# Unit rows by VectorE and their upper parts by ScalarE; a PSUM bank for each task and the last norm's transposes behind down products, in a fused attention and feed-forward kernel

## The chip, the cores and the metric

The kernel runs on one core of one Trainium2 chip. The time is the device time of one execution in microseconds; a verdict compares the kernel before and the changed kernel by such times. TensorE (PE in the profile) multiplies matrices, VectorE (DVE) and ScalarE (ACT) do element-wise work and can read PSUM, the banks that TensorE writes; GpSimd (POOL) does element-wise work on SBUF only; SyncE (SP) issues the DMAs.

## The reference

For each of 16 sequences of 128 tokens with 256 features, cross attention with 32 heads of 8 and then a gated feed-forward layer of 704 hidden units with integer weights, both added to x through a tanh gate:

```python
def _rmsnorm(t):
    return t * jax.lax.rsqrt(jnp.mean(t * t, axis=-1, keepdims=True) + EPS)
q = _rmsnorm(heads(layernorm(x) @ Wq.T)); k = _rmsnorm(heads(context @ Wk.T)); v = heads(context @ Wv.T)
attn = jax.nn.softmax(jnp.einsum('bhnd,bhmd->bhnm', q, k) * scale, axis=-1)
x = x + jnp.tanh(g_xattn[0]) * einsum(attn, v)
gate = silu(_qlinear(layernorm(x), wq_gate, s_gate)); up = _qlinear(layernorm(x), wq_up, s_up)
x = x + jnp.tanh(g_ffn[0]) * _qlinear(gate * up, wq_down, s_down)
```

(`heads` stands here for the reshape into 32 heads.)

## The kernel before

A tile is one sequence (128 tokens by 256 features); the 16 tiles make 8 pairs (`PAIRS`), since the feed-forward layer works on 256 tokens at once. Each engine runs its own list of instructions, written out by hand as an `iteration(p)` for p = -1 to 9 (p = 3 to 5 are a loop, the others are unrolled); semaphores join the lists. An iteration has two halves, e = 0 and e = 1, one for each tile of the pair. It is software pipelined: iteration p projects queries and keys of tiles 2p+2 and 2p+3, does the attention of tiles 2p and 2p+1 in four octets of heads each, normalises tiles 2p-1 and 2p for the feed-forward layer, does chunks 0 and 1 of the feed-forward layer (`ffn0`, `ffn1`) of pair p-1, and chunks 2 to 5 and the down products (`y0`, `y1`) of pair p-2. So iteration 8 has no projections and scores left, and iteration 9 only the last pair's chunks 2 to 5 and its down products. In those two the kernel drains.

Operands of the large products are split into an upper part of reduced precision and a lower part (the rest), and each product is made of both. For queries and keys the chain is: TensorE projects (line 1326); ScalarE squares (`square`) and copies (`copy_qk`, L658, to `qk_raw`); VectorE sums the squares (L942), adds epsilon and takes the inverse root in an 8-step chain `root_y` (L903, L809 to L815) that also holds the layer norm's variance; `normalize2` (L915) writes `x1n`, the normalised tile for the feed-forward layer; `normalize` (L858) writes `xn` for a later tile's queries. Then the unit rows are made twice from `qk_raw` and `root_y`: by VectorE as f16 into `qk_parts` (`qk_upper`, L955), and by GpSimd in full precision into `qk_unit` (`qk_norm`, L530). GpSimd subtracts the two (`split_qk`, L476), VectorE doubles the parts (`qk_double`, L967 and L969), and two transposing DMAs of SyncE bring them to `q_stack` and `k_stack`, from which TensorE takes the scores most of an iteration later.

For each chunk of the feed-forward layer TensorE fills a bank (L1392), ScalarE takes the tanh (L686), VectorE makes `silu2` (`gate`, L1018) and `hidden` (`up`, L1034, which frees the bank), ScalarE rounds it (`upper`, L697) and GpSimd makes the lower part (`split_hidden`, L488). The down products (L1421, L1439) need both parts.

GpSimd's list in the second half of an iteration is, in order: `qk_norm`, `split_qk`, then for two finished tiles a scaling and an addition (`add_y`, L516 and L518), then `add_attention` (L507) for the next iteration's first tile, for whose statistics VectorE waits (L1005).

PSUM has eight banks: four for scores (`score_ps`), one for the weighted values (`pv_ps`), and three that go round among 17 tasks by the table `BANK_OF`. `claim` makes TensorE wait until the task before in the same bank has been drained. In iterations 8 and 9 that table is the same, though nobody needs the four score banks any more. `keep_warm(n)` issues n products of an identity matrix that nobody reads.

## Time and profile before

| what | value |
|---|---|
| median of 3 runs | 254.87 us (253.89 to 255.37) |
| the profiled execution's own time | 252.63 us |
| its span, first to last instruction | 250.4 us |
| mean granted TensorE clock | 0.923 of full |
| busy: PE, DVE, ACT, POOL | 209.6, 193.1, 165.0, 121.9 us |

The profiled execution lies 0.5% below the fastest of the three runs; 2.2 us of its time lie outside the span. PEclk is the clock that TensorE was granted, 1.00 being 2.4 GHz and 0.50 being 1.2 GHz. Matmuls overlap, so PE's busy time says when it worked, not how hard.

### The profile page before, as it was taken

What the parts mean: (1) busy time and instruction counts of PE and PEld (TensorE: products, weight loads), DVE (VectorE), ACT (ScalarE), POOL (GpSimd) and SP (SyncE); (2) the same over time, 40 slices, a digit from 0 to 9 for tenths busy, and PEclk for the clock granted to TensorE, in tenths of its full rate; (3) what the DMA queues carried; (4) which work ended last, traced back from release to release, by engine and by line L of the source; (5) the groups of instructions that cost most, each with busy time, mean ns of one, the idle gap of its engine ahead of it and who ended that gap; (6) DMA issues with size and microseconds to landing.
All of it is one profiled execution on the core that took longest, in us unless ns stands there. A gap on an engine that the chain in (4) does not pass through costs nothing.

```text
span 250.4 us, 7077 instructions
## 1 busy us (share of the span) xinstructions
PE 209.6 (84%) x2536; PEld 171.3 (68%) x2536; DVE 193.1 (77%) x574; ACT 165.0 (66%) x311; POOL 121.9 (49%) x160
## 2 busy tenths in 40 slices
PE   7694875688399899979997999799998998982973
PEld 7592753466178687849885888588777876862963
DVE  4799499798976989696959795969698977686163
ACT  4458599466258886785588768755987588553260
POOL 6211343423424645755484649462946473644442
PEclk9996599589779999997999999979999999997699
DMA  5999405040807040604050405040623150000001
GB/s 168 286 395 339 94 3 85 5 82 7 86 3 86 1 86 1 130 3 84 3 127 0 83 0 126 0 83 1 63 65 67 19 116 16 23 23 0 21 22 45
DMA packets 39692, 17.82 MB, mean 71 GB/s; under 512 B 32752, under 2 KB 39024, under 8 KB 39536
## 3 DMA queue, kind: packets, MB, share of 16 engines
q1 hardware_dynamic: 39664, 17.45, 31.3%
q8 instruction: 18, 0.29, 0.5%
q14 instruction: 10, 0.08, 0.1%
HBM read 7.48 MB, written 2.10 MB: 38 GB/s over the span
## 4 chain that ended last, share of the span: by engine, by line
DVE 36%; PE 27%; issue 17%; POOL 8%; ACT 6%; DMA 2%; SPq 2%; DVEq 1%; POOLq 0%; ACTq 0%
PE bank L1326 8%; PE pv_ps L1294 5%; PE bank L1421 4%; PE bank L1392 4%; DVE sums L942 4%; DVE hidden L1034 3%; DVE qk_parts L955 3%; DVE silu L1018 3%; POOL y_sb L516 2%; DMA w_raw<-w_qkv_dram 2%; POOL x_all L507 2%; PE bank L1362 2%; PE score_ps L1275 2%; DVE root_y L811 2%; DVE root_y L903 2%
## 5 line engine op out<-in xcount | busy, mean ns | idle before, releaser
L594 ACT ACTIVATE probs<-score_ps 128x1024 f32<-128x1024 f32 x64 | 66.1, 1035 | 5.8 <-PE score_ps L1275 5.8
L1294 PE MATMUL pv_ps<-probs,v_blocks 128*32 128x128 f32 x1024 | 43.3, 287 | 8.8 <-ACT probs L594 5.9
L1392 PE MATMUL bank<-x_hi,gu_hi 128*128 128x256 f32 x176 | 46.8, 301 | 2.0 <-DVE hidden L1034 2.0
L530 POOL TENSOR_TENSOR qk_unit<-qk_raw,root_y 128x512 f32<-128x512 f32 x15 | 17.4, 1158 | 57.7 <-DVE root_y L815 57.7
L1392 PE MATMUL bank<-x_lo,gu_hi 128*128 128x256 f32 x176 | 44.0, 285 | 0.0
L488 POOL TENSOR_TENSOR h_lo<-hidden,h_hi 128x256 fp32r<-128x256 f32 x40 | 31.3, 794 | 15.9 <-ACT h_hi L697 15.9
L1392 PEld LDWEIGHTS bank<-x_hi,gu_hi 128*128 128x128 f32 x176 | 34.3, 195 | 6.1 <-issue 2.6
L1294 PEld LDWEIGHTS pv_ps<-probs,v_blocks 128*32 128x32 f32 x1024 | 25.0, 112 | 16.3 <-ACT probs L594 9.1
L1326 PE MATMUL bank<-w_hi,xc_hi 128*128 128x256 f32 x96 | 31.7, 330 | 3.5 <-POOL w_lo L559 1.8
L1392 PEld LDWEIGHTS bank<-x_lo,gu_hi 128*128 128x128 f32 x176 | 34.3, 195 | 0.0
L686 ACT ACTIVATE tanh_g<-bank,half_gate 128x256 f32<-128x256 f32 (+1 forms) x48 | 22.7, 472 | 17.3 <-PE bank L1392 15.5
L1275 PE MATMUL score_ps<-q_stack,k_stack 32*128 32x128 f16 x512 | 26.0, 223 | 5.4 <-ACT k_stack L777 3.2
L1326 PE MATMUL bank<-w_lo,xc_hi 128*128 128x256 f32 x96 | 29.6, 309 | 0.0
L1326 PE MATMUL bank<-w_hi,xc_lo 128*128 128x256 f32 x96 | 29.5, 308 | 0.0
L1018 DVE SCALAR_TENSOR_TENSOR silu<-tanh_g,bank 128x256 f32<-128x256 f32 (+1 forms) x48 | 19.9, 416 | 11.3 <-ACT tanh_g L686 10.7
L1275 PEld LDWEIGHTS score_ps<-q_stack,k_stack 32*128 32x128 f16 x512 | 14.8, 95 | 19.2 <-issue 12.9
L1326 PEld LDWEIGHTS bank<-w_hi,xc_hi 128*128 128x128 f32 x96 | 20.7, 215 | 7.8 <-DVE xc_lo L932 2.5
L1034 DVE SCALAR_TENSOR_TENSOR hidden<-silu,scales,bank 128x256 f32<-128x256 f32 (+1 forms) x48 | 23.0, 480 | 2.0
L476 POOL TENSOR_TENSOR qk_parts<-qk_unit,qk_parts 128x512 f16<-128x512 f32 x15 | 17.6, 1172 | 13.7 <-DVE qk_parts L955 13.6
L1421 PE MATMUL bank<-dn_hi,h_hi 128*128 128x256 f32 x84 | 23.8, 317 | 0.0
L697 ACT CAST h_hi<-hidden 128x256 fp32r<-128x256 f32 (+1 forms) x48 | 18.4, 407 | 8.2 <-DVE hidden L1034 7.8
L1326 PEld LDWEIGHTS bank<-w_hi,xc_lo 128*128 128x128 f32 x96 | 20.9, 218 | 0.0
(105 smaller groups left out, 440.6 us busy)
## 6 DMA issues: line engine op xcount, KB each, us to landing
out_dram<-x_all SPq DMA_DIRECT2D x16, 128.0 KB, 2.0
gu_int<-w_gu_dram SPq DMA_DIRECT2D x1, 1536.0 KB, 8.8
x_all<-x_dram SPq DMA_DIRECT2D x1, 1280.0 KB, 14.4
ctx_sb<-ctx_dram SPq DMA_DIRECT2D x1, 1280.0 KB, 17.5
w_raw<-w_qkv_dram SPq DMA_DIRECT2D x3, 256.0 KB, 3.3
dn_int<-w_dn_dram SPq DMA_DIRECT2D x1, 768.0 KB, 10.1
x_all<-x_dram SPq DMA_DIRECT2D x2, 256.0 KB, 5.3
ctx_sb<-ctx_dram SPq DMA_DIRECT2D x1, 512.0 KB, 6.5
```

The lines of the kernel that those rows point to most:

```text
L476: nc.gpsimd.tensor_tensor(lower_parts(), qk_unit[:].rearrange("p (s h) d -> p s h d", s=2), qk_parts[:, :, 0, :].rearrange("p (s h) d -> p ...
L488: nc.gpsimd.tensor_tensor(lower, hidden[of, j % 3, :], h_hi[of, j, :].bitcast(F32), ALU.subtract).then_inc(h_lo_ready, 1)
L594: nc.scalar.activation(probs[:, t % 2, :], score_ps[t % 2][:].rearrange("p h n -> p (h n)"), ACT.Exp, scale=float(HD) ** 0.5 / UNIT ** 2). ...
L686: nc.scalar.activation(tanh_g[0:r, j % 2, :], bank[k][0:r, 0:TOK], ACT.Tanh, scale=half_gate[0:r, j:j + 1]).then_inc(tanh_g_ready, 1)
L697: nc.scalar.copy(h_hi[of, j, :], hidden[of, j % 3, :]).then_inc(h_hi_ready, 1)
L1018: nc.vector.scalar_tensor_tensor(out=silu2[hidden_rows(j), j % 2, :], in0=tanh_g[0:r, j % 2, :], scalar=1.0, in1=bank[k][0:r, 0:TOK], op0= ...
L1034: nc.vector.scalar_tensor_tensor(out=hidden[of, j % 3, :], in0=silu2[of, j % 2, :], scalar=scales[of, 2, j:j + 1], in1=bank[k][of, half], ...
L1275: last = nc.tensor.matmul(score_ps[t % 2][:, s, :], k_stack[of, e, g, :], q_stack[of, e, g, :], start=True, stop=True, tile_position=(BLOC ...
L1294: last = nc.tensor.matmul(pv_ps[BLOCK * quadrant:BLOCK * (quadrant + 1), region * P:(region + 1) * P], v_blocks[:, e, h * BLOCK:(h + 1) * ...
L1326: last = nc.tensor.matmul(dst, a[:, tile, KC * source + c, :], w[:, column, c, :], start=(n == 1), stop=(n == 3 * KC))
L1392: last = nc.tensor.matmul(bank[k][:, a * TOK:(a + 1) * TOK], w[:, j, a, c, :], xx[:, c, :], start=(n == 1), stop=(n == (4 if wide_weights ...
L1421: last = nc.tensor.matmul(bank[k][:, 0:D], hh[:, j, e * P:(e + 1) * P], w[:, j, :], start=(j == 0 and n == 0), stop=(j == NJ - 1 and n == ...
```

## The change

It has two parts.

1. **Unit rows.** `qk_norm` moves from GpSimd to VectorE, where it takes the place of `qk_upper`: VectorE writes `qk_unit` (f32) once, and ScalarE rounds it to f16 into `qk_parts` with a new `qk_hi`. On ScalarE that copy stands, for e = 0, behind the first exponential of the second half and ahead of chunk 5's tanh; for e = 1, between the tanh of chunk 0 and that of chunk 1. In the second half VectorE's `qk_norm` now stands ahead of `normalize` instead of behind it.
2. **The last two iterations.** TensorE's lists for p = 8 and 9 are replaced by one, `last_pairs`. The four score banks join the ring of three (`NBANK` = 7, `LAST_BANK_OF`). Pair 6's down products now stand partly ahead of `turn2(8)` (the transposes of the last pair's `x1n`) and partly around chunks 0 and 1 of the last pair; 6 warm-up products stand ahead of `turn2(8)` and 5 behind it. VectorE takes all seven root steps of tile 15 in one piece and writes `x1n` ahead of chunks 3 and 4; `turn2_lo` comes ahead of chunk 5. Pair 6's outputs are scaled and added by VectorE at the very end (`add_last_pairs`) instead of by ScalarE and GpSimd.

```diff
-WARM = (14, 14)
+WARM = (14, 14, 6, 5)
...
+    RING, NBANK = 3, 7
+    LAST_BANK_OF = ({"out0": 2, "ffn2": 1, "ffn3": 3, "ffn4": 0, "ffn5": 4, "turn2": 2, "y0": 5, "y1": 6, "ffn0": 1, "ffn1": 3},
+                    {"ffn2": 0, "ffn3": 4, "ffn4": 2, "ffn5": 1, "y0": 3, "y1": 0})
...
+            def qk_hi(p, e):
+                b = 2 * p + e
+                if not has_tile(p, b + 2) or isinstance(b, int) and b == -2:
+                    return
+                act.wait_ge(unit_ready, b + 3)
+                if since(b, -1):
+                    act.wait_ge(stacked, 32 * (b + 2))
+                nc.scalar.copy(qk_parts[:, :, 0, :], qk_unit[:]).then_inc(qk_hi_ready, 1)
...
                 exp_octet(p, 1, 0)
+                if not (isinstance(p, int) and p == FIRST):
+                    qk_hi(p, 0)
                 tanh_chunk(p, 2, 5)
...
                 tanh_chunk(p, 1, 0)
+                qk_hi(p, 1)
                 tanh_chunk(p, 1, 1)
...
-            def qk_upper(p, e):
+            def qk_norm(p, e):
...
                 if since(b, -1):
-                    dve.wait_ge(stacked, 32 * (b + 2))
-                nc.vector.tensor_tensor(qk_parts[:, :, 0, :], qk_raw[:], root_y[:, 0:2 * H].unsqueeze(2).to_broadcast([P, 2 * H, HD]),
-                                        ALU.mult).then_inc(qk_hi_ready, 1)
+                    dve.wait_ge(qk_lo_ready, b + 2)
+                nc.vector.tensor_tensor(qk_unit[:], qk_raw[:], root_y[:, 0:2 * H].unsqueeze(2).to_broadcast([P, 2 * H, HD]),
+                                        ALU.mult).then_inc(unit_ready, 1)
...
+            def last_pairs(wide_weights):
+
+                p = PAIRS
+                weigh(p, 0, 0)
+                out_rows(p, 0)
+                for j in (2, 3, 4, 5):
+                    chunk(p, j, wide_weights)
+                down_part(p, (0, 1, 2), wide_weights)
+                keep_warm(WARM[2])
+                turn2(p)
+                keep_warm(WARM[3])
+                chunk(p, 0, wide_weights)
+                down_part(p, (3, 4), wide_weights)
+                chunk(p, 1, wide_weights)
+                down_part(p, (5,), wide_weights)
+                for j in (2, 3, 4, 5):
+                    chunk(p + 1, j, wide_weights)
+                down_part(p + 1, (0, 1, 2, 3), wide_weights)
+                down_part(p + 1, (4,), wide_weights)
+                down_part(p + 1, (5,), wide_weights)
```

`down_part(p, chunks, ...)` makes the products of these chunks for both tiles of the pair, and waits for each chunk's lower part.

How the rows stand on the engines now. ScalarE, iteration 6, around the first exponential of the second half; before:

```order
L594 ACTIVATE probs<-score_ps1 128x1024
L697 CAST h_hi<-hidden 128x256
L686 ACTIVATE tanh_g<-bank0,half_gate 128x256
L602 COPY o_turned<-pv_ps 128x384
L594 ACTIVATE probs<-score_ps0 128x1024
L686 ACTIVATE tanh_g<-bank1,half_gate 64x256
```

and of the change, the same place:

```order
L590 ACTIVATE probs<-score_ps1 128x1024
L702 CAST h_hi<-hidden 128x256
L691 ACTIVATE tanh_g<-bank0,half_gate 128x256
L598 COPY o_turned<-pv_ps 128x384
L590 ACTIVATE probs<-score_ps0 128x1024
L663 CAST qk_parts<-qk_unit 128x64x8
L691 ACTIVATE tanh_g<-bank1,half_gate 64x256
```

The rounding copy of the unit rows stands between the exponential and chunk 5's tanh, and so ahead of the turned tile (`xc_hi`) and of the next exponential too.

VectorE, iteration 8, from the roots of tile 15 on (L1018 and L1034 are `gate` and `up` of chunks 3, 4 and 5; L1051 is `turn2_lo`); before:

```order
L811 SCALAR_TENSOR_TENSOR root_y<-root_v,root_y 128x65
L1034 SCALAR_TENSOR_TENSOR hidden<-silu2,scales,bank2 128x256
L812 SCALAR_TENSOR_TENSOR root_xy<-root_in,root_y 128x65
L813 SCALAR_TENSOR_TENSOR root_v<-root_xy,root_y 128x65
L814 SCALAR_TENSOR_TENSOR root_p<-root_v 128x65
L815 SCALAR_TENSOR_TENSOR root_y<-root_p,root_y 128x65
L915 SCALAR_TENSOR_TENSOR x1n<-x_all,x1_mean_var,root_y 128x256
L1018 SCALAR_TENSOR_TENSOR silu2<-tanh_g,bank0 128x256
L1034 SCALAR_TENSOR_TENSOR hidden<-silu2,scales,bank0 128x256
L1018 SCALAR_TENSOR_TENSOR silu2<-tanh_g,bank1 64x256
L1034 SCALAR_TENSOR_TENSOR hidden<-silu2,scales,bank1 64x256
L1051 TENSOR_TENSOR x2_lo<-bank1,x2_hi 128x512
```

and of the change (L926 writes `x1n`, L1029 and L1045 are `gate` and `up`, L1062 is `turn2_lo`):

```order
L824 SCALAR_TENSOR_TENSOR root_v<-root_xy,root_y 128x65
L825 SCALAR_TENSOR_TENSOR root_p<-root_v 128x65
L826 SCALAR_TENSOR_TENSOR root_y<-root_p,root_y 128x65
L926 SCALAR_TENSOR_TENSOR x1n<-x_all,x1_mean_var,root_y 128x256
L1029 SCALAR_TENSOR_TENSOR silu2<-tanh_g,score_ps0 128x256
L1045 SCALAR_TENSOR_TENSOR hidden<-silu2,scales,score_ps0 128x256
L1029 SCALAR_TENSOR_TENSOR silu2<-tanh_g,bank0 128x256
L1045 SCALAR_TENSOR_TENSOR hidden<-silu2,scales,bank0 128x256
L1062 TENSOR_TENSOR x2_lo<-bank2,x2_hi 128x512
L1029 SCALAR_TENSOR_TENSOR silu2<-tanh_g,score_ps0 64x256
L1045 SCALAR_TENSOR_TENSOR hidden<-silu2,scales,score_ps0 64x256
```

`gate` and `up` of chunk 3 went from between the root steps to behind `x1n`, and `turn2_lo` went from behind chunk 5 to ahead of it.

TensorE, iteration 8, around the transposes of the last pair's `x1n`, which write bank 1 right behind chunk 5 in the same bank; before:

```order
L1392 MATMUL bank1<-x2_hi,gu_hi 128x256
L1392 MATMUL bank1<-x2_lo,gu_hi 128x256
L1373 MATMUL bank1<-ident,x1n 128x128 x4
L1421 MATMUL bank2<-dn_hi,h_hi 128x256
L1421 MATMUL bank2<-dn_hi,h_lo 128x256
L1421 MATMUL bank2<-dn_hi,h_hi 128x256
```

and of the change, where `score_ps1` holds pair 6's outputs and bank 2 the transposes:

```order
L1449 MATMUL score_ps1<-dn_hi,h_hi 128x256
L1449 MATMUL score_ps1<-dn_hi,h_lo 128x256
L1254 MATMUL pv_ps<-ident 128x128 x6
L1386 MATMUL bank2<-ident,x1n 128x128 x4
L1254 MATMUL pv_ps<-ident 128x128 x5
L1405 MATMUL bank1<-x2_hi,gu_hi 128x256
L1405 MATMUL bank1<-x2_lo,gu_hi 128x256
```

Twelve down products and six warm-up products stand ahead of the transposes now, and chunk 0 of the last pair comes behind five more warm-up products instead of behind all 22 down products.

## Rows read from the trace of the kernel before

**Rows 1.** Windows: stretch, length, busy of PE, PEld, DVE, ACT, POOL, then PEclk, DMA.

```profile
78.78:103.68 24.90, 23.76 (x316) 19.40 (x313) 21.40 (x73) 19.35 (x38) 14.83 (x19) 1.00 0.24 42
103.68:130.26 26.58, 24.52 (x309) 20.24 (x309) 20.59 (x58) 18.66 (x38) 15.60 (x19) 0.94 0.31 65
130.26:155.32 25.06, 23.46 (x313) 19.18 (x312) 20.39 (x57) 19.22 (x39) 15.10 (x19) 1.00 0.25 48
155.32:180.96 25.64, 23.89 (x305) 19.57 (x304) 20.15 (x58) 18.03 (x38) 14.85 (x19) 0.93 0.28 43
230.00:235.70 5.70, 5.67 (x27) 5.67 (x28) 0.69 (x1) 1.36 (x3) 2.43 (x4) 0.50 0.00 0
235.70:246.70 11.00, 9.09 (x67) 8.09 (x66) 5.41 (x12) 5.45 (x13) 5.88 (x8) 0.99 0.08 26
```

**Rows 2.** Timeline of VectorE, iteration 4: start us, duration us, instruction, [idle before].

```profile
134.30 1.35 DVE L915 SCALAR_TENSOR_TENSOR x1n<-x_all,x_mean_var,root_y 128x256 f32<-128x256 f32 x1
...
146.93 1.31 DVE L858 SCALAR_TENSOR_TENSOR xn<-x_all,x_mean_var,x_root_y 128x256 f32 x1
...
155.32 0.69 DVE L942 TENSOR_REDUCE sums<-squares 128x64 f32<-128x512 f32 x1 [0.29 <-issue]
```

**Rows 3.** Timeline of TensorE, iteration 4.

```profile
137.78 0.55 PE L1362 MATMUL bank<-ident,o_turned 128*128 128x128 f32 x3 [0.84 <-DVE hidden L1034]
```

**Rows 4.** Timeline of GpSimd, iteration 4.

```profile
134.29 1.08 POOL L530 TENSOR_TENSOR qk_unit<-qk_raw,root_y 128x512 f32<-128x512 f32 x1 [3.04 <-DVE root_y L815]
...
148.91 1.16 POOL L476 TENSOR_TENSOR qk_parts<-qk_unit,qk_parts 128x512 f16<-128x512 f32 x1 [0.96 <-DVE qk_parts L955]
...
153.29 0.73 POOL L507 TENSOR_TENSOR x_all<-x_all,attn 128x256 f32 x1
```

**Rows 5.** Timeline of ScalarE, iterations 4 and 5.

```profile
135.08 1.03 ACT L594 ACTIVATE probs<-score_ps 128x1024 f32<-128x1024 f32 x1
...
147.64 0.48 ACT L686 ACTIVATE tanh_g<-bank,half_gate 128x256 f32<-128x256 f32 x1 [0.61 <-PE bank L1392]
...
174.21 0.47 ACT L686 ACTIVATE tanh_g<-bank,half_gate 128x256 f32<-128x256 f32 x1 [0.61 <-PE bank L1392]
```

**Rows 6.** Groups by line: count, busy us, mean ns, idle before.

```profile
L1018 DVE SCALAR_TENSOR_TENSOR silu<-tanh_g,bank 128x256 f32<-128x256 f32 (+1 forms) x48 | 19.9, 416 | 11.3 <-ACT tanh_g L686 10.7
...
L697 ACT CAST h_hi<-hidden 128x256 fp32r<-128x256 f32 (+1 forms) x48 | 18.4, 407 | 8.2 <-DVE hidden L1034 7.8
...
L658 ACT COPY qk_raw<-bank 128x512 f32<-128x512 f32 x16 | 9.4, 590 | 0.0
...
L1102 DVE TENSOR_TENSOR qk_unit<-qk_raw,root_y 128x512 f32<-128x512 f32 x1 | 0.7, 691 | 0.0
```

**Rows 7.** Timeline of VectorE, iterations 8 and 9.

```profile
227.67 0.49 DVE L915 SCALAR_TENSOR_TENSOR x1n<-x_all,x_mean_var,root_y 128x256 f32<-128x256 f32 x1
...
229.49 0.49 DVE L1034 SCALAR_TENSOR_TENSOR hidden<-silu,scales,bank 64x256 f32<-64x256 f32 x1
231.87 0.69 DVE L1051 TENSOR_TENSOR x_lo<-bank,x_hi 128x512 fp32r<-128x512 f32 x1 [1.90 <-ACT x_hi L705]
...
244.43 0.49 DVE L1034 SCALAR_TENSOR_TENSOR hidden<-silu,scales,bank 64x256 f32<-64x256 f32 x1
246.71 0.75 DVE L1060 TENSOR_TENSOR y_sb<-bank,down_scale 128x256 f32<-128x256 f32 x2 [1.80 <-PE bank L1439]
```

**Rows 8.** Timeline of TensorE, the last pair's transposes.

```profile
230.03 1.12 PE L1373 MATMUL bank<-ident,x1n 128*128 128x128 f32 x4 [4.64 <-DVE hidden L1034]
```

**Rows 9.** Chain that ended last, end of iteration 8: start, duration, what.

```profile
231.15 4.69 PE bank L1421 x22
235.84 1.01 PE bank L1392 x8
```

**Rows 10.** Timeline of GpSimd, chunk 2's lower part in iteration 8.

```profile
225.11 0.72 POOL L488 TENSOR_TENSOR h_lo<-hidden,h_hi 128x256 fp32r<-128x256 f32 x1 [0.96 <-ACT h_hi L697]
```

**Rows 11.** Timeline of TensorE, its second warm-up of 14 products.

```profile
14.57 3.29 PE L1241 MATMUL pv_ps<-ident 128*128 128x128 f32 x28
```

More of the change, by code:

```diff
@@ L549, in iteration @@
                 context_lo(p + 1, 0)
-                qk_norm(p, 1)
                 split_qk(p, 1)
@@ L766, in iteration @@
                 context_hi(p + 1, 0)
+                if isinstance(p, int) and p == PAIRS:
+                    turn2_hi(p)
                 upper(p, 2, 5)
@@ L781, in iteration @@
                     power_ffn(2)
-                turn2_hi(p)
+                if not (isinstance(p, int) and p == PAIRS):
+                    turn2_hi(p)
                 drain_y(p, 0)
@@ L1213, in iteration @@
                     roots(p, 1, 1, 4)
-                    turn2_lo(p)
+                    if not (isinstance(p, int) and p == PAIRS):
+                        turn2_lo(p)
                     roots(p, 1, 5, 7)
                 normalize2(p, 1)
+                qk_norm(p, 1)
                 normalize(p, 1)
                 weight_pieces(p, 1, 0)
-                qk_upper(p, 1)
                 gate(p, 1, 0)
```

101 lines of the change are left out of this document (45 added, 56 removed).

## The prediction

> **What bounds the kernel now.** I read the windows first, one for each iteration, since busy shares over the whole span mix stages [rows 1]. Iterations 2 to 5 last 24.9, 26.6, 25.1 and 25.6 us. No engine fills them: VectorE is busy 20 to 21 us, ScalarE 18 to 19, GpSimd about 15. TensorE shows 23.5 to 24.5, but two of the four had a clock below 1.00, and these are the two long ones. So an iteration is a chain through all engines. I follow it through iteration 4, from one sum of squares (130.26, 25.06 us before the next at 155.32) to the other:
>
> - sum to TensorE's `out_rows` at 137.78, 7.52 us of roots, `x1n` and chunks 3 and 4 on VectorE; TensorE waited 0.84 us there for VectorE's `up` of chunk 4, whose bank it needs [rows 3]
> - from there TensorE's own queue to chunk 0's tanh at 147.64, 9.86 us; ScalarE waited for TensorE [rows 5]
> - tanh to GpSimd's `split_qk` at 148.91, 1.27 us; then six operations of GpSimd to `add_attention` at 153.29, 4.38 us; then 2.03 us to the next sum [rows 2, 4].
>
> In it two VectorE rows stand out: `x1n` took 1.35 us and `xn` 1.31, where the same shape takes 0.49 at the end of the kernel [rows 2, 7]. Both ran beside GpSimd's `qk_norm`; the first began 0.01 us behind it, and that took 1.08 us [rows 4]. So each `qk_norm` of GpSimd stops VectorE for about 0.85 us, in the first half on the chain.
>
> The end is another regime. TensorE idles 4.64 us until 230.03 [rows 8], and in 230.0 to 235.7 it runs at half clock, 0.50, which is 1.2 GHz [rows 1]. The timelines and the chain of waits say why: the transposes for the last pair wait for bank 1, which `up` of chunk 5 frees at 229.98, though `x1n` was written at 228.16; they and 22 down products then take 5.8 us, and only behind them comes chunk 0 of the last pair [rows 7 to 9]. From there chunks share three banks and TensorE and VectorE take turns until the last `up` ends at 244.92 [rows 7].
>
> **Part 1, unit rows.** Removed: 15 `qk_norm` of GpSimd, 1.08 us or more each. VectorE keeps a multiplication of the same size (0.69 us where it once writes `qk_unit` [rows 6]). Added: 15 roundings of 128x512 on ScalarE. No row has exactly that; the nearest is `copy_qk`, 0.59 us, and half the size from SBUF takes 0.41 [rows 6]. I take 0.5 us from start to start; bounds 0.41 and 0.82 (twice the half).
>
> The Trainium skill (ScalarE: Activation LUTs, Rules for kernel authors) gives about 0.3 us and 0.83 ns for each element: an estimate of 0.72 us. By it the part would give 0.2 us less in each half that the copy ends.
>
> First half. `x1n` gets its 0.85 us back. But GpSimd, no longer held by `qk_norm`, now takes chunk 2's lower part (0.72 us [rows 10]) as `x1n` runs or right behind it, and VectorE's `qk_norm` reads two SBUF tiles as `x1n` does; if it is stopped in turn, 0.35 to 0.45 us is lost again. So 0.4 to 0.9 us sooner at chunk 4's `up`, and I take 0.5, since TensorE waits there. ScalarE's copy comes just in time: the exponential ahead of it ends at 136.11 [rows 5], the unit rows would be ready at about the same time. Behind it chunk 5's tanh and the next exponential are 0.5 us later; TensorE's 9.9 us of queued work covers the exponential.
>
> Second half. `split_qk` no longer waits for the stalled `xn` and the multiplication behind it, but for tanh 0 (0.47) and the copy (0.5) on ScalarE: 1.05 us with the hand-overs, where it was 1.27 in iteration 4 (gain 0.2). In iteration 5, where TensorE was late, tanh to the next sum was 180.96 - 174.21 = 6.75 us [rows 1, 5]; the new path is 1.05 + 4.38 + 2.03 = 7.46, a loss of 0.7.
>
> So an iteration at full clock would last 25.06 - 0.5 - 0.2 = 24.35 us. Iterations 2 to 5: 0.55 + 2.2 + 0.7 + 1.3 = 4.8 us gained if the clock stays up in all four; 0.6 + 0.5 + 0.7 + 0 = 1.8 if it falls in 3 and 5 as now. The idle stretch ahead of the fall shrinks but is not gone; I count one of two falls as saved: 3.2 us. Iteration 6, the last that makes unit rows, I count at nothing, like iteration 5 under its own clock. Iterations -1 to 1 too: there the copy stands on ScalarE ahead of exponentials that are due before the unit rows, which costs what VectorE gets back; bounds -0.7 to +0.7. The transposing DMAs start up to 0.5 us later or sooner, with some 8 us until their scores.
>
> **Part 2, the end.** Up to `out_rows` of iteration 8 nothing moves. Then:
>
> - `x1n`: `gate` and `up` of chunk 3 (0.42 and 0.49 with their hand-overs) no longer stand between the roots: it ends at about 227.1 instead of 228.16 [rows 6, 7].
> - TensorE: chunks 2 to 5 come without bank waits; of pair 6's first 12 down products eight wait for chunk 2's lower part, which ended at 225.83 [rows 10] and which I put at 226.0, and take 1.0 us, to 227.0; six warm-up products at 3.29/14 = 0.235 us each [rows 11] take it to 228.4; transposes to 228.9. Late by 1.3 us against `x1n`, at no cost:
> - VectorE first does chunks 3 and 4, 4 operations at 0.42 to 0.49, to 228.9, and ScalarE rounds chunk 4 (0.41, to 229.35) before `turn2_hi` (0.6, as `copy_qk`, which has its size) and VectorE's `turn2_lo` (0.69): 230.7 [rows 6, 7]. The five warm-up products (1.2 us) fill most of this wait.
> - chunk 0 starts at 230.7; its eight products ended the 22 down products at 235.84 before [rows 9]: 5.1 us sooner, less 0.2 for the overlap, 4.9.
> - from there: chunk 0 (1.01 us for eight products [rows 9], 0.12 each), 8 down products, chunk 1, 2 down products: 233.9. The last two need chunk 5's lower part; VectorE's `up` of it ends at 231.6, rounding and lower part make it 232.85, in time. Then 28 products of chunks 2 to 5, to 237.3, no bank awaited. Chunk 2 is full at 235.05, its tanh (0.47) done at 235.55, and VectorE trails from there with 0.94 for each of four chunks (`gate` 0.42, `up` 0.49 and hand-overs; ScalarE's 0.88 for each fits in): the last `up` ends at 239.35 against 244.92 [rows 7].
> - behind it the same steps: rounding, lower part, last products, four operations of VectorE, store. What pair 6's outputs cost ScalarE (two copies) and GpSimd (four operations) before lay beside the half-clock products and gives nothing. Its four operations on VectorE (1.5 us) fall into the 1.80 us in which it waits for TensorE [rows 7]; its two stores are issued ahead of the last two.
>
> Part 2 gives 5.5 us.
>
> **Sum.** 3.2 + 5.5 = 8.7 us off the profiled execution's 252.63. The median of the runs shown stands 2.24 above it, and I put the gain to the median: 254.87 - 8.7 = 246.2 us.
>
> **Rivals.**
>
> - *The end only* (0.18): part 1 gives nothing, since VectorE's new `qk_norm` is stopped by the lower part of chunk 2 for its whole length and ScalarE's copy is on the path in the second half (+0.7 in each iteration as in iteration 5). 254.87 - 5.5 = 249.4. For it: GpSimd's queue ends both halves. Against it: 0.85 us is lost now, at most 0.73 then. The Trainium skill (SBUF — State Buffer, Who interferes with whom) has it as an exclusive lock: a VectorE operation with two SBUF inputs and a GpSimd operation that reads SBUF stop each other for the whole instruction, whoever is second; the rows agree (1.35 against 0.49).
> - *The clock falls at the end as well* (0.13): TensorE waits about 1 us ahead of the down products and 0.8 ahead of chunk 0. Before, it idled 4.64 us and then had half clock for 5.7 [rows 1, 8]. If it falls again, the 22 products of chunk 0, of chunk 1 and between them, and some of the next, take 0.21 instead of 0.12: 2.3 us back, 248.5.
> - *The clock stays up everywhere* (0.14): 4.8 + 5.5 and 0.5 from the first iterations: 244.1.
> - *Slower* (0.03): all of ScalarE's 15 copies land on the chain, since everything behind them on ScalarE (exponentials, then TensorE's weighing) moves, and neither VectorE nor GpSimd's gain is used: 15 x 0.6 = 9.0 - 5.5 = 3.5 us, 258.4. It decides from 5.5/15 = 0.37 us a copy. ScalarE is idle 6 us in each iteration, much of it waiting for TensorE, which speaks against it.
>
> The forecast itself has 0.50, with a range of its own of 244.6 to 248.0; 0.02 is for what I don't see. The range 243.3 to 250.3 takes in the first three rivals and the bounds: part 1 from 0 to 5.5, part 2 from 3.2 to 6. A measurement of this kernel tells about 0.5%, 1.3 us, from no change. Faster by more than that 0.95, within it 0.02, slower 0.03.
>
> **What would show it.** `x1n` at 0.5 us in the first half; `qk_norm` of VectorE between 0.7 and 1.2; iterations of 24.0 to 24.6 us at full clock; `split_qk` about 1.05 us behind the start of tanh 0; PEclk 1.00 behind the last transposes; chunk 0 of the last pair some 15 us ahead of the last instruction; the last `up` 5.5 us ahead of the end, as before. Wrong would be: VectorE waiting for ScalarE's copy by way of GpSimd at `qk_double`, exponentials late by more than TensorE's slack, or a window of 0.50 at the end.

## The result, and the profile after

The changed kernel took 244.70 us (median of 4 runs, 242.47 to 246.10), the kernel before in the same session 254.38 (4 runs, 252.96 to 255.37). The ratio is 0.9615, 95% interval 0.9519 to 0.9712: faster by 9.7 us. The profiled execution of the changed kernel was its slowest, 246.10 us with a span of 244.3; that of before was 252.63 with 250.4.

In the profile after, `x1n` is line 926, VectorE's `qk_norm` 966, ScalarE's `qk_hi` 663, GpSimd's `split_qk` 487 and `split_chunks` 499, `gate` 1029, `up` 1045, `turn2_hi` 710, `turn2_lo` 1062, the transposes of `turn2` 1386, the chunks' products 1405, those of `down_part` 1449, the warm-ups 1254.

The windows of the changed kernel, with the columns of [rows 1]: iterations 2 to 5, and the last stretch, from the three products of the last `out_rows` to the end.

```profile
82.82:106.72 23.90, 22.99 (x315) 18.84 (x309) 19.48 (x72) 19.86 (x40) 12.86 (x17) 1.00 0.28 52
106.72:131.32 24.60, 23.68 (x318) 19.56 (x315) 18.95 (x58) 20.42 (x41) 13.53 (x18) 1.00 0.30 63
131.32:156.79 25.47, 24.34 (x308) 19.91 (x307) 18.25 (x57) 19.39 (x39) 12.59 (x17) 0.93 0.25 49
156.79:180.37 23.58, 22.70 (x308) 18.56 (x307) 18.52 (x57) 19.43 (x40) 12.46 (x17) 1.00 0.27 46
219.76:244.30 24.54, 18.52 (x145) 17.41 (x145) 17.27 (x45) 9.32 (x23) 9.51 (x13) 1.00 0.08 27
```

Iterations 2 to 5 take 97.55 us where they took 102.18 [rows 1]: 4.63 less, and one of them still has a clock below 1.00. The last stretch was 29.91 us before (220.49 to the end at 250.40) and is 24.54: 5.37 less, at full clock. That makes 10.0. Iteration 6 and what follows it up to the last `out_rows` gives 0.14 (39.53 and 39.39). But the spans of the two profiled executions differ by 6.1 only, since iteration 2 begins 4.04 us later: at 82.82 instead of 78.78.

VectorE in iteration 4, to be held against [rows 2]; columns: start, duration in us, instruction.

```profile
135.36 0.48 DVE L926 SCALAR_TENSOR_TENSOR x1n<-x_all,x_mean_var,root_y 128x256 f32<-128x256 f32 x1
...
136.16 0.83 DVE L966 TENSOR_TENSOR qk_unit<-qk_raw,root_y 128x512 f32<-128x512 f32 x1
...
137.44 0.48 DVE L1045 SCALAR_TENSOR_TENSOR hidden<-silu,scales,bank 128x256 f32<-128x256 f32 x1
```

`x1n` takes 0.48 instead of 1.35 us. The new `qk_norm` takes 0.83. From the sum (131.32) to the end of chunk 4's `up` (137.92) it is 6.60 us; before it was 7.46 (130.26 to 137.72). GpSimd, against [rows 4]:

```profile
135.48 0.97 POOL L499 TENSOR_TENSOR h_lo<-hidden,h_hi 128x256 fp32r<-128x256 f32 x1 [3.44 <-ACT h_hi L702]
```

The lower part of chunk 2, 0.73 us elsewhere, takes 0.97 here, beside `x1n` and `qk_norm`. GpSimd is held up a little and VectorE hardly.

TensorE at the end, against [rows 8, 9]; the warm-ups (line 1254) are written as two rows each:

```profile
226.24 1.50 PE L1254 MATMUL pv_ps<-ident 128*128 128x128 f32 x12
227.57 0.60 PE L1386 MATMUL bank<-ident,x1n 128*128 128x128 f32 x4
228.01 1.28 PE L1254 MATMUL pv_ps<-ident 128*128 128x128 f32 x10
230.08 0.36 PE L1405 MATMUL bank<-x_hi,gu_hi 128*128 128x256 f32 x1 [0.79 <-DVE x_lo L1062]
```

Chunk 0 of the last pair starts 14.2 us ahead of the span's end and was 14.8 ahead before (235.64); the last `up` ends 5.5 us ahead of it in both (238.76 of 244.3, 244.92 of 250.4). So the gain of the end lies ahead of chunk 0 (4.8 us) and in the alternation of TensorE and VectorE behind it (0.6 us), and nothing of it is lost later.

Where the 4 us went shows TensorE in iteration 1, before (first fence) and after. "issue" is time in which the profile shows nothing that it waited for.

```profile
61.60 0.60 PE L1373 MATMUL bank<-ident,x1n 128*128 128x128 f32 x4
64.48 0.40 PE L1275 MATMUL score_ps<-q_stack,k_stack 32*128 32x128 f16 x8 [2.27 <-issue]
...
67.95 0.37 PE L1294 MATMUL pv_ps<-probs,v_blocks 128*32 128x128 f32 x1 [2.36 <-issue]
```

```profile
62.42 0.60 PE L1386 MATMUL bank<-ident,x1n 128*128 128x128 f32 x4
66.95 0.29 PE L1288 MATMUL score_ps<-q_stack,k_stack 32*128 32x128 f16 x2 [3.92 <-issue]
70.02 0.50 PE L1288 MATMUL score_ps<-q_stack,k_stack 32*128 32x128 f16 x6 [2.79 <-issue]
```

Here TensorE comes to the branch on `any_wide`. Before, it stood twice, 2.27 and 2.36 us; after, 3.92 and 2.79, and the second pause now falls into the first eight score products, so that ScalarE's exponential and `turn2_hi` behind it wait for both (ScalarE is idle for 6.86 us there). I had not read these rows for the prediction.

### The profile page after: what moved, and what is told of

Its sections match the earlier page's. It is cut to its first block, busy times and chain, and to the rows that moved or that the text cites. A ratio compares the mean times of both kernels' runs of the same rounds, so it can differ in the third digit from the quotient of the medians.

```text
span 244.3 us, 7106 instructions
## 1 busy us (share of the span) xinstructions
PE 208.2 (85%) x2558; PEld 171.0 (70%) x2558; DVE 183.1 (75%) x578; ACT 170.8 (70%) x324; POOL 102.4 (42%) x141
## 4 chain that ended last, share of the span: by engine, by line
DVE 30%; PE 29%; issue 18%; POOL 9%; ACT 7%; DMA 2%; SPq 2%; DVEq 1%; POOLq 1%; ACTq 0%
PE bank L1339 8%; PE bank L1405 6%; PE pv_ps L1307 5%; PE bank L1434 4%; DVE sums L953 3%; POOL y_sb L527 3%; DVE qk_unit L966 3%; POOL qk_parts L487 3%; DVE hidden L1045 2%; DMA w_raw<-w_qkv_dram 2%; POOL x_all L518 2%; DVE silu L1029 2%; PE score_ps L1288 2%; ACT probs L590 2%; DVE root_y L914 1%
## 5 line engine op out<-in xcount | busy, mean ns | idle before, releaser
L1307 PE MATMUL pv_ps<-probs,v_blocks 128*32 128x128 f32 x1024 | 44.0, 293 | 8.2 <-ACT probs L590 8.1
L1405 PE MATMUL bank<-x_hi,gu_hi 128*128 128x256 f32 x162 | 43.6, 302 | 0.8 <-DVE x_lo L1062 0.8
L1405 PE MATMUL bank<-x_lo,gu_hi 128*128 128x256 f32 x162 | 41.3, 289 | 0.0
L1405 PEld LDWEIGHTS bank<-x_hi,gu_hi 128*128 128x128 f32 x162 | 31.9, 197 | 4.3 <-issue 3.5
L1405 PEld LDWEIGHTS bank<-x_lo,gu_hi 128*128 128x128 f32 x162 | 32.0, 198 | 0.0
L691 ACT ACTIVATE tanh_g<-bank,half_gate 128x256 f32<-128x256 f32 (+1 forms) x44 | 20.8, 473 | 11.4 <-PE bank L1405 10.4
L1029 DVE SCALAR_TENSOR_TENSOR silu<-tanh_g,bank 128x256 f32<-128x256 f32 (+1 forms) x44 | 18.3, 416 | 8.5 <-ACT tanh_g L691 8.3
L1045 DVE SCALAR_TENSOR_TENSOR hidden<-silu,scales,bank 128x256 f32<-128x256 f32 (+1 forms) x44 | 21.1, 480 | 1.9
L1339 PEld LDWEIGHTS bank<-w_lo,xc_hi 128*128 128x128 f32 x96 | 20.8, 216 | 0.0
L1016 DVE BATCH_NORM_STATS2 x_stats<-x_all 128x6 f32<-128x256 f32 (+1 forms) x16 | 6.8, 425 | 18.2 <-POOL x_all L518 18.2
```

What stands on the lines that cost most here:

```text
L691: nc.scalar.activation(tanh_g[0:r, j % 2, :], bank[k][0:r, 0:TOK], ACT.Tanh, scale=half_gate[0:r, j:j + 1]).then_inc(tanh_g_ready, 1)
L1029: nc.vector.scalar_tensor_tensor(out=silu2[hidden_rows(j), j % 2, :], in0=tanh_g[0:r, j % 2, :], scalar=1.0, in1=bank[k][0:r, 0:TOK], op0= ...
L1045: nc.vector.scalar_tensor_tensor(out=hidden[of, j % 3, :], in0=silu2[of, j % 2, :], scalar=scales[of, 2, j:j + 1], in1=bank[k][of, half], ...
L1307: last = nc.tensor.matmul(pv_ps[BLOCK * quadrant:BLOCK * (quadrant + 1), region * P:(region + 1) * P], v_blocks[:, e, h * BLOCK:(h + 1) * ...
L1339: last = nc.tensor.matmul(dst, a[:, tile, KC * source + c, :], w[:, column, c, :], start=(n == 1), stop=(n == 3 * KC))
L1405: last = nc.tensor.matmul(bank[k][:, a * TOK:(a + 1) * TOK], w[:, j, a, c, :], xx[:, c, :], start=(n == 1), stop=(n == (4 if wide_weights ...
```

## The experiments

All twelve were read for the same quantities, so they stand in one table; each is explained below. Iteration lengths run from one first sum of squares to the next; the last column from the last `out_rows` to the end of the span. All in us, from the profiled execution of each; median and ratio to the kernel before over all its runs. The ratio is to the kernel before in the same session as the run; its median was 254.38 us in the session of after, 254.14 in that of part1_only, part2_only, turn2_early and no_branch, 254.09 in that of hi_first, warm_after, both and no_warm, and 253.63 in that of gps_unit, vec_both, narrow_first and best.

```
kernel          it. 1   it. 2   it. 3   it. 4   it. 5   end     median  ratio (95%)
before          24.88   24.90   26.58   25.06   25.64   29.91   254.38
after           28.33   23.90   24.60   25.47   23.58   24.54   244.70  0.9615 (0.9519-0.9712)
part1_only      26.13   23.90   24.63   24.01   23.59   29.58   247.78  0.9764 (0.9704-0.9824)
part2_only      26.47   24.92   26.60   25.08   25.61   24.58   249.50  0.9839 (0.9784-0.9894)
gps_unit        27.83   24.06   24.27   24.19   23.75   24.57   244.28  0.9610 (0.9528-0.9692)
vec_both        26.49   24.57   25.04   24.67   24.23   24.52   245.94  0.9708 (0.9633-0.9782)
turn2_early     26.49   23.87   24.61   24.00   23.58   27.00   246.33  0.9713 (0.9661-0.9766)
no_warm         25.92   23.87   24.63   24.04   23.58   26.05   244.22  0.9640 (0.9558-0.9723)
hi_first        26.67   23.89   24.64   24.03   23.60   24.27   243.59  0.9610 (0.9540-0.9680)
warm_after      26.83   23.91   24.64   24.01   23.59   24.56   245.44  0.9678 (0.9612-0.9744)
both            26.65   23.88   24.61   24.01   23.58   24.06   242.41  0.9548 (0.9480-0.9615)
no_branch       23.82   23.89   24.62   24.03   23.59   24.52   240.23  0.9452 (0.9405-0.9500)
narrow_first    23.66   23.89   24.63   24.04   23.60   25.50   240.37  0.9480 (0.9408-0.9552)
best            23.67   23.92   24.61   24.04   23.60   24.48   239.43  0.9430 (0.9338-0.9521)
```

Iterations 2 to 5 repeat to a few hundredths in the kernels that share their code (but for iteration 4 of after), which the medians do not: no_warm has the lower median and the longer end against after. What a step is worth is best read in these columns, though each comes from one profiled execution of a kernel. Iteration 1 does not repeat: turn2_early, no_warm, hi_first, warm_after and both have its code unchanged from after.

### Each part alone

part1_only has the diff's unit rows and upper parts and the old end; part2_only the reverse.

> Only part 1 of the change: unit rows by VectorE and upper parts by ScalarE, the last two iterations as before. My theory: iterations 2 to 5 give what they gave with the whole change, 4.6 us by the two traces (x1n 0.48 us instead of 1.40), and the rest nothing, so 254.4 - 4.6 = 249.8 us; with the early loss of 4 us that the trace of after shows in iterations -1 to 1, about 252 to 254. Rival: part 1 gives nothing in the steady iterations and the clock differs by chance between executions; then an iteration at full clock stays at 24.9 us as before, and not 23.6 to 23.9.

> Only part 2: new order and seven banks in the last two iterations, unit rows still by GpSimd and upper parts by VectorE. My theory: the end, from the three products of out_rows of the last iteration to the end of the span, goes from 29.9 to 24.5 us as in after, so 254.4 - 5.4 = 249.0 us. There are no unit rows in these iterations, so part 1 has no share in it. Rival: part of the 5.4 us needs part 1 (GpSimd free earlier); then the end is 25.5 to 27 us long.

The windows of part1_only, iterations 2 to 5:

```profile
80.11:104.01 23.90, 22.98 (x314) 18.85 (x309) 19.48 (x73) 19.87 (x40) 12.87 (x17) 1.00 0.28 47
104.01:128.64 24.63, 23.71 (x319) 19.61 (x316) 18.96 (x59) 20.44 (x41) 13.52 (x18) 1.00 0.30 62
128.64:152.65 24.01, 22.83 (x308) 18.52 (x307) 18.61 (x58) 19.36 (x39) 12.62 (x17) 1.00 0.26 53
152.65:176.24 23.59, 22.70 (x308) 18.57 (x307) 18.52 (x57) 19.42 (x40) 12.45 (x17) 1.00 0.29 41
```

They take 96.13 us, 6.05 less than before, and the clock is 1.00 in all four. In part2_only they take 102.21, as before (102.18), iteration by iteration, with the same two clocks of 0.94 and 0.93. So both falls of before come again where part 1 is left out and are gone with it; and the profiled execution of after, with 97.55, had a fall of its own in iteration 4, which is 1.46 us longer than in part1_only. The end of part2_only is 24.58 us: part 1 has no share in it. The parts are worth 6.05 and 5.3 us in these stretches; in the medians 6.4 and 4.6. Each alone is faster than the kernel before, but neither is clear of a ratio of 0.98 by its interval.

Both rivals fell. Of the times, 249.8 was put for part 1 and 247.78 measured, since its iterations gave 6.05 us where I had put 4.6 from the trace of after, fall included; for part 2 it was 249.0 and 249.50. "About 252 to 254" for part 1 with an early loss fell too: iteration 1 lost 1.25 us there, not 4.

### Which half of part 1

gps_unit keeps ScalarE's upper parts and gives the unit rows back to GpSimd (first piece its queue, then VectorE's, in both halves); vec_both keeps VectorE's unit rows and gives it back the upper parts (VectorE's queue, then ScalarE's):

```diff
                 context_lo(p, 1)
+                qk_norm(p, 0)
                 split_chunks(p, 2, (2,))
...
                 weight_pieces(p, 0, 0)
-                qk_norm(p, 0)
```

```diff
                 exp_octet(p, 1, 0)
-                if not (isinstance(p, int) and p == FIRST):
-                    qk_hi(p, 0)
                 tanh_chunk(p, 2, 5)
...
                 qk_norm(p, 0)
+                qk_upper(p, 0)
```

> Half of part 1: the changed kernel with the unit rows back on GpSimd (two instructions of 1.1 us), the upper parts on ScalarE as in after, so VectorE has neither. Theory 1, that of the prediction (VectorE is stopped in x1n while GpSimd runs the product, and this is what part 1 gives back): x1n again takes 1.36 to 1.40 us in both halves and iterations 2 to 5 are 24.4 to 25.1 us at full clock, against 23.59 to 24.63 with the whole of part 1. Theory 2 (only the work on VectorE between the root steps and the last `up` counts): x1n's stop of 0.9 us takes the place of the product of 0.69 to 0.83 us that has gone from VectorE, and iterations 2 to 5 come within 0.2 us of part 1's.

> The other half: VectorE makes the unit rows and then, as before, the upper parts (0.68 us each); ScalarE makes none of them. Theory: x1n stays at 0.48 us, but VectorE has 0.68 us more in each half, in the first half ahead of `up` of chunk 4, in the second on the way to the upper parts; iterations 2 to 5 are 0.5 to 1.3 us longer than part 1's 23.59 to 24.63 us, and 247 to 250 us in all. Rival: ScalarE, which no longer has the two copies of 0.5 us, gives it back; no change from after.

VectorE in iteration 4 of gps_unit, then of vec_both:

```profile
134.81 1.36 DVE L941 SCALAR_TENSOR_TENSOR x1n<-x_all,x_mean_var,root_y 128x256 f32<-128x256 f32 x1
136.09 0.47 DVE L1047 SCALAR_TENSOR_TENSOR hidden<-silu,scales,bank 128x256 f32<-128x256 f32 x1
...
137.02 0.48 DVE L1047 SCALAR_TENSOR_TENSOR hidden<-silu,scales,bank 128x256 f32<-128x256 f32 x1
```

```profile
134.85 0.48 DVE L914 SCALAR_TENSOR_TENSOR x1n<-x_all,x_mean_var,root_y 128x256 f32<-128x256 f32 x1
...
135.64 0.83 DVE L954 TENSOR_TENSOR qk_unit<-qk_raw,root_y 128x512 f32<-128x512 f32 x1
136.39 0.68 DVE L967 TENSOR_TENSOR qk_parts<-qk_raw,root_y 128x512 f16<-128x512 f32 x1
...
137.53 0.48 DVE L1046 SCALAR_TENSOR_TENSOR hidden<-silu,scales,bank 128x256 f32<-128x256 f32 x1
```

In gps_unit `x1n` is stopped as before in the first half, 1.36 us (in the second half of iterations 3 to 5 it is `xn` that takes 1.30, as in before, and not `x1n`, as I had put). Yet chunk 4's `up` ends 6.72 us behind the sum, against 6.60 after and 7.46 before; iterations 2 to 5 take 96.27 us, 0.14 from part1_only. In vec_both `x1n` is free and `up` ends at 7.24 us, and the four iterations take 98.51. So theory 2 holds: what counts is all that VectorE has between the roots and that `up`. Of vec_both's own numbers, three of four iterations are 0.64 to 0.67 us longer than part 1's (0.5 to 1.3 put) and iteration 3 only 0.41; the 247 to 250 us were too many (245.94), and the rival, no change, fell by the iterations. Before, these were the stop of `x1n` (0.87 us) and one product, the upper part (0.82 us there); in gps_unit the stop alone, after, one product alone, in vec_both two products (0.83 and 0.68). One load instead of two is the gain, whichever is left. The median of gps_unit agrees: 244.28, no difference from after that can be measured.

Each of the two kernels has one half of part 1, so they also say what a half is worth alone against the 102.18 us of before: the unit rows moved to VectorE (vec_both) 3.67 us over four iterations, the upper parts moved to ScalarE (gps_unit) 5.91, both 6.05. In iterations 2 and 4, at full clock in all of them, it is 0.33 and 0.39, 0.84 and 0.87, 1.00 and 1.05. So the halves do not add up, and removing the stop is worth little only where the upper part has gone already.

Neither has a clock below 1.00 in these iterations. Before, TensorE waits twice in a row for `up`, ahead of `xn`'s transposes and ahead of `out_rows`: 1.00 and 0.84 us in iteration 3 and 0.89 and 0.84 in iteration 5, where the clock fell, 0.54 and 0.84 in iteration 4, where it did not. In gps_unit, vec_both and part1_only there is one such wait in each of these iterations: 0.50, 1.10 and 0.70 us in iteration 3, and up to 1.24 (vec_both, iteration 5). A pair of waits as long as that of before goes with the fall there; that it is the cause is not shown, since after had its fall in iteration 4 behind one wait of 0.85 us.

### TensorE's order and the warm-ups of the end

turn2_early is this edit; no_warm sets the last two numbers of WARM, 6 and 5, to 0 and 0, warm_after to 0 and 11:

```diff
+                turn2(p)
                 down_part(p, (0, 1, 2), wide_weights)
                 keep_warm(WARM[2])
-                turn2(p)
```

> The changed kernel, but TensorE again takes the last norm's four transposes ahead of the down products of chunks 0 to 2 (with the warm-ups behind them); banks, VectorE's and ScalarE's order as in after. Theory of the prediction: TensorE then stands idle for 3 us before the transposes, comes out of it at the lower clock, and the twelve down products of 0.21 us each and the first chunk are behind them: x_lo is ready at the same time, the span is 1 to 2.5 us longer than after's. Rival: the gain of the end comes from VectorE's order and the banks alone; then the span is within 0.3 us of after's from the last iteration's out_rows.

> The changed kernel without the eleven warm-ups of the end (the products of the identity with itself, which compute nothing). Theory: TensorE stands idle for 2.5 to 3 us between the transposes and chunk 0, as in the run with the transposes early (3.02 us idle, then 0.21 us for each product), and comes back at the lower clock of 1.2 GHz: the down products and chunks behind it cost 1 to 2.5 us, the end is at 25.5 to 27 us. Rival: the warm-ups are not needed, since the idle stretches are each shorter than before's 4.64 us; the end stays at 24.5 us with products of 0.12 us.

> The changed kernel, with all eleven warm-ups of the end behind the last norm's transposes, none ahead. Theory (ScalarE's queue sets x_hi): the transposes start at 6.9 instead of 7.81 us after the last out_rows, x_hi at 8.80 as before, the end stays at 24.5 us. Rival (the six warm-ups ahead of the transposes hold the chain up by 0.9 us): x_hi at 7.9 and the end at 23.6 us.

TensorE in turn2_early:

```profile
222.50 0.86 PE L1386 MATMUL bank<-ident,x1n 128*128 128x128 f32 x4 [3.02 <-DVE x1n L926]
...
223.38 0.42 PE L1449 MATMUL score_ps<-dn_hi,h_lo 128*128 128x256 f32 x1
...
225.51 0.41 PE L1449 MATMUL score_ps<-dn_hi,h_lo 128*128 128x256 f32 x1
225.73 2.83 PE L1254 MATMUL pv_ps<-ident 128*128 128x128 f32 x22
228.32 0.36 PE L1405 MATMUL bank<-x_hi,gu_hi 128*128 128x256 f32 x1
```

With the transposes ahead TensorE idles 3.02 us, comes back at half clock (0.21 us for a product), and chunk 0 starts 12.72 us behind the last `out_rows` instead of 10.32. The end is 27.00 us, 2.46 longer. That is not the price of the order alone. VectorE's `x_lo`, which chunk 0 needs, is ready as soon as in after, 10.17 us behind the last `out_rows`:

```profile
225.08 0.69 DVE L1062 TENSOR_TENSOR x_lo<-bank,x_hi 128x512 fp32r<-128x512 f32 x1 [1.03 <-ACT x_hi L710]
```

It ends at 225.77, and the last of the twelve down products has begun at 225.51. What stands between that and chunk 0 at 228.32 are the eleven warm-ups, 2.6 us, which this edit puts on the chain; the clock is back at 1.00 from about 226.5. So the run shows the idle stretch and the lower clock behind it, but what the order would cost without the warm-ups is not shown.

It shows a second thing: the transposes begin 0.91 us sooner than in after (6.90 instead of 7.81), but `x_hi` at 8.80, as in after. TensorE in no_warm:

```profile
222.75 0.63 PE L1386 MATMUL bank<-ident,x1n 128*128 128x128 f32 x4 [0.27 <-DVE x1n L926]
226.16 0.36 PE L1405 MATMUL bank<-x_hi,gu_hi 128*128 128x256 f32 x1 [2.79 <-DVE x_lo L1062]
226.35 0.28 PE L1405 MATMUL bank<-x_lo,gu_hi 128*128 128x256 f32 x1
...
227.84 0.41 PE L1449 MATMUL score_ps<-dn_hi,h_hi 128*128 128x256 f32 x1
```

It idles 2.79 us, and here the products behind it are first 0.12 us apart and then 0.21, from about 1.3 us after the return to 230.8. The end is 26.05 us, 1.51 longer. Half clock was not there at once, as I had put it, but the price lies in the expected range; the rival fell. warm_after answers to the letter: transposes at 6.90, `x_hi` at 8.79, end 24.56. So the six warm-ups ahead of the transposes cost nothing.

### ScalarE's queue at the end

hi_first is this edit; both is the same with 0 and 7 for the last two numbers of WARM:

```diff
+                if isinstance(p, int) and p == PAIRS:
+                    turn2_hi(p)
                 upper(p, 2, 4)
                 drain_v(p, 1)
                 context_hi(p + 1, 0)
-                if isinstance(p, int) and p == PAIRS:
-                    turn2_hi(p)
```

> The changed kernel, with ScalarE's copy of the last norm's transposes (x_hi) put ahead of the upper part of chunk 4 in iteration 7 instead of behind it. All times count from the three products of the last out_rows. In after the transposes start at 7.81 and x_hi at 8.80, right behind h_hi of chunk 4; with the transposes taken earlier (6.90) x_hi still began at 8.80. Theory: ScalarE's queue sets x_hi. With this edit alone it can start when the transposes end, at 8.4 to 8.5, so the span's end comes 0.3 us sooner (24.2 us). Rival: x_hi waits for the transposes or VectorE alone; no change, 24.5 us.

> The changed kernel with both edits: no warm-up ahead of the last norm's transposes, seven behind them, and x_hi ahead of the upper part of chunk 4. Theory: x_hi starts at 8.2 us behind the last out_rows, behind the tanh of chunk 5, x_lo behind `up` of chunk 4 ends at 9.6 instead of 10.17, and the end is 0.6 us sooner (23.9 us). Rival: the clock falls, as fewer warm-ups stand in the gap; then chunk 0's products take 0.21 us each instead of 0.12 and the end is at 24.5 us or later.

ScalarE in after, then in both:

```profile
228.25 0.41 ACT L702 CAST h_hi<-hidden 128x256 fp32r<-128x256 f32 x1
228.56 0.58 ACT L710 CAST x_hi<-bank 128x512 fp32r<-128x512 f32 x1
```

```profile
224.48 0.47 ACT L691 ACTIVATE tanh_g<-score_ps,half_gate 64x256 f32<-64x256 f32 x1
224.85 0.57 ACT L710 CAST x_hi<-bank 128x512 fp32r<-128x512 f32 x1
225.31 0.41 ACT L702 CAST h_hi<-hidden 128x256 fp32r<-128x256 f32 x1
```

`x_hi` waits in after for the upper part of chunk 4, ahead of it in the queue. hi_first starts it at 8.44 (end 24.27 us, 0.27 less), both at 8.31 behind the tanh of chunk 5 (end 24.06, 0.48 less): the theory, with 0.1 us less than I had put for both. Seven warm-ups were enough there: the mean clock of both's last stretch is 1.00.

### The branch on TensorE

no_branch (first piece) leaves out the products for weights over one part's range, and with them the branch and the load of its register; narrow_first (second) leaves nothing out; best is narrow_first with the two edits of both.

```diff
             pe.wait_ge(ffn_hi_ready, 3)
-            pe.wait_ge(wide_steps, 2)
-            any_wide = pe.alloc_register("any_wide")
-            pe.reg_load(any_wide, wide[:])
-            with pe.If_ne(any_wide, 0):
-                attention_last(1, True)
-                first_chunks(1, True)
-                run(pe, lambda p: pair(p, True), 2)
-            with pe.Else():
-                attention_last(1, False)
-                first_chunks(1, False)
-                run(pe, lambda p: pair(p, False), 2)
+            attention_last(1, False)
+            first_chunks(1, False)
+            run(pe, lambda p: pair(p, False), 2)
```

```diff
-            with pe.If_ne(any_wide, 0):
+            with pe.If_eq(any_wide, 0):
+                attention_last(1, False)
+                first_chunks(1, False)
+                run(pe, lambda p: pair(p, False), 2)
+            with pe.Else():
                 attention_last(1, True)
                 first_chunks(1, True)
                 run(pe, lambda p: pair(p, True), 2)
-            with pe.Else():
-                attention_last(1, False)
-                first_chunks(1, False)
-                run(pe, lambda p: pair(p, False), 2)
```

> The changed kernel without the branch on TensorE: it leaves out the products with the weights' lower parts for weights over the integer range that one part holds, which this data does not have. Theory: the two gaps of TensorE in iteration 1 (3.92 and 2.79 us in after, 2.27 and 2.36 us in before) are the code behind the branch being fetched; without it both are gone and the kernel is 6 to 7 us faster than after, about 238 us. Rival: the gap is a wait for data that the profile does not show, or the code is fetched just as late without a branch; then TensorE still stands idle for 4 us or more between 60 and 72 us.

> The changed kernel with the two sides of TensorE's branch exchanged: the products for this data (no lower weight parts) stand first, right behind the branch, the others in the else part. Nothing is left out. Theory: the gaps come from the jump over the other side's code; without a jump the code that follows is there, iteration 1 is 23.8 us as without a branch, and the time is about 240.2 us. Rival: the branch itself, taken or not, or the register load ahead of it makes TensorE fetch its code anew; then the gaps of 3.5 and 2.5 us stay, iteration 1 is 26 to 28 us and the time 243 to 246 us.

> All that helped together: the sides of the branch exchanged, x_hi ahead of the upper part of chunk 4, no warm-up ahead of the last transposes and seven behind them. If the jump theory holds, 240.2 - 0.5 = 239.7 us; if it does not, as in the run with both edits of the end, 242.4 us.

TensorE of narrow_first at the branch:

```profile
61.56 0.60 PE L1386 MATMUL bank<-ident,x1n 128*128 128x128 f32 x4
62.10 0.40 PE L1288 MATMUL score_ps<-q_stack,k_stack 32*128 32x128 f16 x8
62.42 0.65 PE L1307 MATMUL pv_ps<-probs,v_blocks 128*32 128x128 f32 x16
...
67.02 0.55 PE L1405 MATMUL bank<-x_hi,gu_hi 128*128 128x256 f32 x1 [2.56 <-DVE x_lo L1062]
```

Between transposes and scores nothing is left of the pauses; the 2.56 us ahead of chunk 0 is a wait for VectorE's `x_lo`, a matter of data. Iteration 1 is 23.66 us, 23.82 without the branch, and 25.9 to 28.3 in the ten other changed kernels. A branch that is taken over the other side's code costs; the same branch that falls through, with the same wait and register load ahead of it, does not. The rivals of both runs fell. But no_branch took 240.23 us where I had put about 238: its iteration 1 is 4.51 us shorter than after's, not by the 6.71 of the two pauses; without them TensorE waits 2.58 us for `x_lo` instead. narrow_first (240.2 put) and best (239.7 put) came within 0.3 us.

The DMA queues tell the same. In iteration 1 queue q8, whose kind is "instruction", moves 5 packets in before and in each of the ten changed kernels that jump, and 2 in no_branch, narrow_first and best. The Trainium skill (Runtime: NRT & Kernel Launch, Instruction fetch mechanics) says that a taken branch to code outside the window already fetched waits for a fetch by DMA. This case's traces agree; the two pauses are 4.63 to 6.71 us in sum, and iteration 1 is 2.3 to 4.7 us longer than in narrow_first.

The jump did not vanish: narrow_first now has to pass over the other side's code at the end. Its last stretch is 25.50 us, though its last `up` ends where after's does (18.98 and 19.00 us behind the last `out_rows`). The last stores (SyncE's queue), narrow_first and then after, begin alike too, 20.55 and 20.56 us behind it, and take longer:

```profile
233.35 2.81 SPq L439 DMA_DIRECT2D out_dram<-x_all  x4
```

```profile
240.32 2.14 SPq L439 DMA_DIRECT2D out_dram<-x_all  x4
```

DMA queues in the last 6 us of narrow_first (packets, MB, share), then of after:

```profile
q1 hardware_dynamic: 576, 0.52, 26.3%
q8 instruction: 1, 0.02, 1.1%
q14 instruction: 1, 0.01, 0.4%
```

```profile
q1 hardware_dynamic: 576, 0.52, 26.0%
q14 instruction: 1, 0.01, 0.5%
```

One more block of instructions comes in there, beside the last output's store. In best the end is 24.48 us where both had 24.06 (stores 2.61 and 2.14 us), with two more blocks. So 0.4 to 1.0 us of what iteration 1 gains is paid at the end, and all of it behind the last `up`; that the blocks hold the stores up is argued from their standing side by side, and two blocks cost less than one.

The spread is smaller in two of the three: the six runs of no_branch lie within 0.93 us and the four of narrow_first within 0.76, those of the kernels that jump within 1.3 to 3.7. In best it is not: its median is 239.43 us (ratio 0.943, interval 0.934 to 0.952), but one of its four runs took 243.06, at a mean clock of 0.931 against 0.948; it was not profiled, and its cause is open.

## Why the prediction was right, and where it was not

The time, 246.2 us, was 1.5 above the 244.7 measured, with the sum made of one good term, one too small and one that was missing. The last two are of opposite sign, so that the sum came this close (8.7 us off, 9.7 measured) is partly luck.

- **Part 2, 5.5 us: right.** 5.37 in the profile of after, 5.33 in part2_only. The steps held: `x1n` 0.92 us sooner (1.0 put), chunk 0 at 10.32 us behind the last `out_rows` where 230.7 - 220.49 = 10.2 was put, last `up` 5.43 sooner (5.57). How the 5.4 us divide between the seven banks, VectorE's order and TensorE's order was not tried one by one. That the warm-ups ahead of the transposes cost nothing, since ScalarE's rounding of chunk 4 is later, was argued there and is shown by warm_after; that they are needed at all, by no_warm (1.5 us; the rival "the clock falls at the end as well" put 2.3).
- **Part 1, 3.2 us: too small.** It is 6.05. The step that failed first is "0.35 to 0.45 us is lost again" in the first half: `qk_norm` took 0.83 us, 0.14 over its 0.69, and GpSimd's lower part 0.97. The upper part that stood in `qk_norm`'s place before took 0.82 in iteration 4, so that exchange cost VectorE 0.01, not 0.35. The gain at chunk 4's `up` was 0.86 instead of 0.5. The second half held (tanh 0 to `split_qk` 1.06 us, 1.05 put). At full clock iterations 2 and 4 became 1.00 and 1.05 us shorter, 0.7 put for iteration 4. The second step is "I count one of two falls as saved": both went, in every kernel with either half of part 1, and iterations 3 and 5 gave 1.95 and 2.05. The 4.8 with the clock up in all four was too low for the same reasons, and since the loss of 0.7 in iteration 5 did not come. Of the clock the rival "the clock stays up everywhere" (244.1) was nearer: none of the nine other kernels with the whole of part 1 has a fall in iterations 2 to 5, and only after has one. ScalarE's copy took 0.61 us and 0.51 from start to start (149.69 and 150.20 in after), as taken (0.5) and not the estimated 0.72. Two slips change nothing: 25.06 - 0.5 - 0.2 is 24.36, and the products of chunk 0, of chunk 1 and between them are 24, not 22.
- **The reason given for part 1 was half of it.** I put the gain down to `x1n`, stopped by GpSimd's product. For the exchange as a whole that sum is right: VectorE had 1.35 + 0.82 us before and 0.48 + 0.83 after, 0.86 less, and `up` of chunk 4 came 0.86 sooner. But gps_unit keeps the stop, drops the product instead, and has nearly the whole gain (1.36 + 0), and vec_both, which only removes the stop, has a part (0.48 + 0.83 + 0.68). The prediction had the rows for this and did not add up VectorE's stretch. The lock that the Trainium skill describes (SBUF — State Buffer, Who interferes with whom) is seen in `x1n`, 1.35 and 1.36 us in before and gps_unit beside GpSimd's product and 0.48 in after without it; that the lower part of chunk 2 would stop VectorE for its whole length, the rival "the end only", is not: the two overlap for 0.3 us (136.16 to 136.45 in after), and VectorE lost 0.14 us there, GpSimd 0.24.
- **Iterations -1 to 1, "bounds -0.7 to +0.7": wrong.** In the profiled after they cost 4.04 us, 3.45 of it in iteration 1, at the jump. Every changed kernel that jumps has a longer iteration 1 (25.9 to 28.3 against 24.88), with pauses of 5.28 to 6.71 us in sum against 4.63. Part of after's 28.33 belongs to that execution and not to the change: turn2_early, no_warm, hi_first, warm_after and both have the same code there and took 25.92 to 26.83. The two longest, after and gps_unit (27.83), are also the ones with the lower mean clock in that iteration, 0.82 against 0.87 in the eight others. What makes the pauses of all of them dearer than before's stays open: before was profiled once, in an execution 1.8 us below its median, and part2_only, whose iteration 1 is otherwise that of before, took 26.47, so the unit rows alone are not the reason.

The 9.7 us of the medians are less than 6.05 + 5.3 = 11.4; some 1.7 us are lost. The early jump and a fall of the clock like that in iteration 4 are the two losses that the traces show; how often each comes in the runs without a profile is not known.

## What to carry to other kernels

When an instruction is stopped by a neighbour, the question is not what the stop costs but what the engine has to do in all between two hand-overs: here, removing the stop by taking over the neighbour's work was worth 3.67 us over four iterations alone and 0.14 once a third operation had gone to an engine with slack, and handing that operation over was worth 5.91 alone. Look at the copy that follows a transpose before adding or removing work ahead of the transpose. And read the first third of a trace too: a branch on a value that is nearly always the same should fall through to the common side, which gave some 4 us by exchanging two blocks (240.37 against 244.70 us, in two sessions; against the kernel before of its own session 13.3 us off instead of 9.7).
